# Opening steps of both mixture-of-experts stages reordered in a Flamingo-style block kernel

## The chip, the cores and the metric

The kernel is written in Bass, with every engine's instruction list and every semaphore set by hand. It runs on one core of one Trainium2 chip. The metric is the device time of the whole program in microseconds (us); less is better. Five engines work side by side: PE (TensorE, with PEld for its weight loads), DVE (VectorE), ACT (ScalarE), POOL (GpSimd) and SP (SyncE, which here only issues DMAs; SPq is its queue).

## The reference

x is 128 sequences of 64 rows of 128 numbers, 8192 rows in all. Four layers follow each other, and each adds a gated attention and a gated feed-forward part to x. The two feed-forward parts that matter here are mixtures of eight experts with two chosen per row. The first (layer 0) normalises x, takes logits against `gate_w`, and gives the two largest a softmax weight; every expert is one 128x128 matrix. The second (layer 2) is this:

```python
logits = jnp.einsum('bne,ec->bnc', x, Wr) + br
probs = jax.nn.softmax(logits, axis=-1)
topk_probs, topk_idx = jax.lax.top_k(probs, TOP_K)
...
combine = jnp.einsum('tk,tke->te', flat_w, onehot)
out = jnp.zeros_like(flat_x)
for ei in range(NUM_EXPERTS):
    h = jax.nn.gelu(flat_x @ W1[ei] + b1[ei], approximate=False)
    y = h @ W2[ei] + b2[ei]
    out = out + combine[:, ei:ei + 1] * y
...
x = x + jnp.tanh(g_ffn[0]) * _L0_ffn_ref(_layernorm(x, axis=-1), L0_ffn_gate_w, L0_ffn_We)
x = x + jnp.tanh(g_ffn[2]) * _L2_ffn_ref(_layernorm(x, axis=-1), L2_ffn_Wr, ...)
```

Both kernels compute every expert for every row and multiply by the coefficient, which is zero where the expert was not chosen.

## The kernel before

x stays on the chip for the whole run, as 64 tiles of 128 rows. Eight stages come one after another: attention0, experts0, attention1, spiking1, attention2, experts2, attention3, quantised3. Each stage begins on every engine with a wait for the last row update of the stage before, so a stage that ends earlier lets all that follows start earlier.

A mixture stage goes over 16 groups of 4 tiles (512 rows) in a software pipeline. A loop written out by hand calls `body(at)` for each step s, and `at(k)` is group s+k, or nothing where that group does not exist. So `at(4)` is a group four steps ahead of the one whose outputs are made, and the first steps, in which `at(0)` is nothing, are the opening: only their front parts have work. Every engine works through its own `body` strictly in the order of the text, and waits where a semaphore says so. The order of the work is nothing but these lists.

**First mixture, experts0 (lines 830 to 1008), opening steps -4 to -1.** A group goes through these stations:
- DVE takes the statistics of its four tiles (L712, L718); POOL turns the variances into 1/sqrt (L738, L741); DVE makes the shift -mean/sigma (L972); ACT makes the normalised rows (L1000); PE transposes them (L917) and ACT copies the result to xT (L1005).
- One step later PE makes the logits (L901). DVE copies them (L926) and runs `top_two` (L695 to L705, L932); ACT makes two sigmoids of the gap (L989); DVE makes the coefficients (L937, L942).
- One step later PE transposes the coefficients (L908) and ACT copies them (L994, the "ct copy"). SP stores them to DRAM (L864, 16 KB), waits until they are there, and issues the spread (L868), which brings them back to all 128 partitions (2048 KB in SBUF).
- One step later DVE weighs: xT times the spread coefficients, eight instructions of 128x512 (L952). Then PE sums over the experts (L888, `outputs`) and DVE updates x (L963).

Before the change DVE's `body` has the order statistics of the new group, update of the old one, `top_two`, shift of the new group, first three weighings, coefficients, other five. ACT has sigmoids, ct copy, normalised rows, xT copy. PE has outputs of the first tile, logits, transpose of the coefficients, outputs of the other three tiles, transposes of the new group.

**Second mixture, experts2 (lines 1579 to 1779), opening steps -3 to -1.** It is the same idea with three groups ahead. `t_front` and `a_front` (L749, L754) transpose a normalised group and copy it. `scores` (L1683 to L1688) follows the logits (L1655), ACT makes the exponential (L1768), and `routing` (L1694 to L1708) ends in the coefficients, which PE transposes (L1668). ACT's ct copy is L1774, the store L1609, the spread L1613. PE then multiplies the coefficients with the output bias (L1673) into the bank that the next group's logits use, and DVE adds it to x (L1749, semaphore `b2_added`). The inner layer has 12 chunks: PE `hidden` (L1633, three chunks per call, three banks in turn), ACT the Gelu out of the bank (`hidden_out`, L1758), DVE the product with the coefficients (`weigh`, L1720). PE's `outputs` is L1643. On PE `t_front` stands at the end of each step and `hidden` in quarters q = 0 to 3, with the transpose of the coefficients behind q = 1. On ACT the ct copy stands behind the third quarter's Gelus and `a_front` at the end of the step. On DVE the statistics, the first weighing and the normalised rows (L202) of the new group all stand ahead of `routing`.

Of the kernel before, what the change touches and what calls it, by code (L numbers as in the profile page):

```python
# [20 lines left out]
P = 128  # L21
# [808 lines left out]
def experts0(k, no):  # L830
# [50 lines left out]
    def tensor(pe):  # L881
# [11 lines left out]
        def body(at):  # L893
            if g := at(0):
                outputs(g, 0)
            if g := at(3):
# [7 lines left out]
            if g := at(2):  # L904
                pe.wait_ge(*s["coef"](g))
                if g.has(1):
                    pe.wait_ge(*s["ct_sb"](g.back(1)))
                pe.transpose(ps[0:COLS, COEFT, 0:P], coef[g.par], k.ident).then_inc(s["ct_psum"].sem, 1)  # L908
# [12 lines left out]
    def vector(dve):  # L921
# [22 lines left out]

        def weigh(g, first, last):
# [9 lines left out]
        def body(at):  # L955
# [5 lines left out]
            if old:  # L961
# [3 lines left out]
                    .then_inc(f["x_updated"].sem, GROUP)  # L965
            if far:
                top_two(far)
            if new:
                dve.wait_ge(*f["rstd_ready"](sub(new, GROUP - 1)))
                if new.has(1):  # L970
                    dve.wait_ge(*f["xhat_ready"](sub(new.back(1), GROUP - 1)))
                dve.scalar_tensor_tensor(out=shift, in0=k.mv[:, :, 0, 0], scalar=-1.0, in1=k.rstd[:, :, 0],  # L972
                                         op0=ALU.mult, op1=ALU.mult).then_inc(s["shift"].sem, 1)
# [8 lines left out]
    def scalar(act):  # L982
        def body(at):
            if g := at(3):
                act.wait_ge(*s["gap"](g))
                if g.has(1):
                    act.wait_ge(*s["part"](g.back(1)))
                for n in range(2):
                    act.activation(share[:, n], gap, ACT.Sigmoid, scale=2.0 * n - 1.0).then_inc(s["share"].sem, 1)  # L989
            if g := at(2):  # L990
# [3 lines left out]
                act.activation(coefT[g.par][0:COLS, :], ps[0:COLS, COEFT, 0:P], ACT.Copy).then_inc(s["ct_sb"].sem, 1)  # L994
            if g := at(4):
# [583 lines left out]
def experts2(k, no):  # L1579
# [44 lines left out]
    def tensor(pe):  # L1624
# [23 lines left out]
        def body(at):  # L1648
            g, nxt, far = at(0), at(1), at(2)
            if far:  # L1650
# [25 lines left out]
            if at(3):  # L1676
                t_front(pe, at(3))
        steps(pe, G, 3, 0, body)

    def vector(dve):  # L1680
# [41 lines left out]

        def body(at):
            old, nxt, far, new = at(-1), at(1), at(2), at(3)
            if far:
                scores(far)
# [453 lines left out]
```

## Time and profile before

| what | value |
|---|---|
| time, 3 runs | median 2242.03 us, 2236.01 to 2242.62 |
| the profiled execution | 2245.91 us, span 2244.1 us |
| mean granted clock of TensorE | 0.944 of full speed |
| PE busy | 1965.8 us, 88% of the span |
| DVE busy | 1700.4 us, 76% |
| ACT busy | 1192.8 us, 53% |
| POOL busy | 262.5 us, 12% |
| experts0 in the span | about 672 to 853 us |
| experts2 in the span | about 1378 to 1795 us |

"Busy" is the time in which an engine worked on an instruction, "idle" what lies between. In a timeline row stand the start in us, the duration, the engine, the line, the operation, output <- input with shapes, the count of merged instructions, and in brackets the idle time before it with what ended it. A windows row has the stretch, its length, then busy time and count of PE, PEld, DVE, ACT and POOL, the granted clock of PE (1.00 is 2.4 GHz, 0.50 is 1.2 GHz), the DMA share and GB/s. A wait marked "issue" has no releaser that the profile could name. Matmul times are modelled at their ends, and a matmul in float32 stands there as two instructions.

### The profile page before, as it was taken

Reading aid. Unit: us, or ns where it says so; the run is one execution under the profiler, and the core shown is the slowest. Engines: PE = TensorE matmul, PEld = TensorE weight load, DVE = VectorE, ACT = ScalarE, POOL = GpSimd, SP = SyncE. Lnnn points to the kernel's source line nnn. Section 1 sums busy time; section 2 is a strip of 40 time slices with the busy share of each in tenths; the row PEclk is TensorE's granted clock in tenths of the full one; section 3 lists DMA queues with packets and bytes.
Section 4 is the critical chain, followed back from the end, with each engine's and each line's share of the span. In section 5 each row is a group of like instructions: output and inputs, shape, how many; then the busy total and the mean of one; then the engine's idle time right before and its main releaser. Section 6 shows DMA issues by size and latency. Waiting matters only on the chain. (4 is left out here: it accounts for less than half of the span.)

```text
span 2244.1 us, 48290 instructions
## 1 busy us (share of the span) xinstructions
PE 1965.8 (88%) x18173; PEld 1522.7 (68%) x18173; DVE 1700.4 (76%) x4753; ACT 1192.8 (53%) x2324; POOL 262.5 (12%) x553
## 2 busy tenths in 40 slices
PE   3999999999986998999989886999999986499808
PEld 3788888888876897777757665577777765244307
DVE  2787887878866887999967786766666668787894
ACT  1555555555543215888866553544454445316844
POOL 0011111011101101111111142000000022200000
PEclk9999999999997998999989998999999998699958
DMA  6222221212213551111100011222221111001462
GB/s 184 50 49 49 51 50 47 51 49 50 51 32 152 227 228 26 32 33 30 33 8 1 10 48 55 78 77 103 87 76 76 76 43 34 0 1 72 172 205 76
DMA packets 123591, 155.71 MB, mean 69 GB/s; under 512 B 47561, under 2 KB 104290, under 8 KB 119266
## 3 DMA queue, kind: packets, MB, share of 16 engines
q1 hardware_dynamic: 117368, 149.92, 20.8%
q8 instruction: 147, 2.41, 0.5%
q10 hardware_dynamic: 5994, 2.70, 0.4%
q14 instruction: 82, 0.67, 0.1%
HBM read 110.11 MB, written 25.69 MB: 61 GB/s over the span
## 5 line engine op out<-in xcount | busy, mean ns | idle before, releaser
L1720 DVE TENSOR_TENSOR arena<-arena 128x512 f32<-128x512 f32 (+1 forms) x256 | 170.7, 685 | 68.9 <-ACT arena L1758 64.8
L1758 ACT ACTIVATE arena<-banks,b1c 128x512 f32<-128x512 f32 x192 | 131.7, 687 | 170.4 <-PE banks L1633 170.2
L1643 PEld LDWEIGHTS banks<-w2a,arena 128*128 128x128 f32 x1024 | 124.1, 192 | 28.6 <-issue 28.6
L888 PE MATMUL banks<-we,arena 128*128 128x128 f32 x1024 | 132.9, 284 | 4.4 <-DVE arena L952 0.5
L491 PE MATMUL banks<-arena,wk 128*128 128x128 f32 x1024 | 134.5, 286 | 1.1 <-DVE arena L609 1.1
L888 PEld LDWEIGHTS banks<-we,arena 128*128 128x128 f32 x1024 | 122.5, 195 | 12.8 <-DVE arena L952 12.4
L491 PEld LDWEIGHTS banks<-arena,wk 128*128 128x128 f32 x1024 | 122.1, 196 | 12.4 <-issue 10.7
L1643 PE MATMUL banks<-w2a,arena 128*128 128x128 f32 x1024 | 124.7, 275 | 0.0
L595 DVE TENSOR_TENSOR arena<-arena,konst 128x512 f32<-128x512 f32 x64 | 44.3, 693 | 104.3 <-DMA arena<-arena 104.3
L1633 PE MATMUL banks<-arena,w1s 128*128 128x512 f32 x256 | 122.1, 611 | 0.0
L501 PE MATMUL banks<-wv,arena 128*128 128x512 f32 x256 | 120.9, 595 | 0.0
L638 ACT ACTIVATE arena<-banks 128x512 f32<-128x512 f32 x64 | 38.2, 597 | 142.0 <-PE banks L491 142.0
L202 DVE TENSOR_SCALAR xhat<-x_tiles,mean_var,rstd 128x128 f32<-128x128 f32 x256 | 79.2, 341 | 34.5 <-POOL rstd L741 26.4
L738 POOL TENSOR_SCALAR var_eps<-mean_var 128x4 f32<-128x4 f32 x96 | 22.0, 229 | 702.7 <-DVE mean_var L718 700.5
L741 POOL TENSOR_TENSOR rstd<-var_eps,konst 128x4 f32<-128x4 f32 x96 | 100.1, 1043 | 15.3 <-POOL var_eps L738 11.7
L1850 PE MATMUL banks<-konst,local_max 128*1 128x128 f32 (+1 forms) x4 | 1.4, 348 | 111.0 <-DVE local_max L1834 111.0
L632 ACT ACTIVATE arena<-arena 128x512 f32<-128x512 f32 x128 | 80.6, 630 | 25.7 <-DVE arena L579 24.9
L1893 PE MATMUL banks<-arena,wup 128*128 128x512 f32 x192 | 92.0, 617 | 0.8 <-ACT arena L2051 0.8
L579 DVE TENSOR_TENSOR arena<-banks,arena 128x512 f32<-128x512 f32 x128 | 88.5, 691 | 4.4
L1198 ACT ACTIVATE arena<-arena 128x512 f32<-128x512 f32 x128 | 80.7, 630 | 16.2 <-DVE arena L1152 11.4
L1147 DVE TENSOR_REDUCE arena<-banks 128x8 f32<-128x512 f32 x128 | 87.3, 682 | 2.4 <-PE banks L1084 2.3
L952 DVE TENSOR_TENSOR arena<-arena 128x512 f32<-128x512 f32 x128 | 79.6, 686 | 10.9 <-issue 9.4
(271 smaller groups left out, 5091.5 us busy)
## 6 DMA issues: line engine op xcount, KB each, us to landing
arena<-coef_scratch SPq DMA_DIRECT2D x32, 2048.0 KB, 7.2
arena<-arena SPq DMA_DIRECT2D x256, 64.0 KB, 2.0
gated_scratch<-arena SPq DMA_DIRECT2D x16, 768.0 KB, 3.2
arena<-gated_scratch SPq DMA_DIRECT2D x16, 768.0 KB, 4.4
arena<-z1T_scratch SPq DMA_DIRECT2D x128, 64.0 KB, 2.4
arena<-ctxT_scratch SPq DMA_DIRECT2D x32, 256.0 KB, 2.8
arena<-in_ctx SPq DMA_DIRECT2D x64, 64.0 KB, 1.9
z1T_scratch<-arena SPq DMA_DIRECT2D x64, 64.0 KB, 1.7
```

The source lines that it names most:

```text
L491: mm = pe.matmul(ps[:, n, c * P:(c + 1) * P], k.wk0[:, c * P:(c + 1) * P], Z[t.par][:, :, n], start=True, stop=True)
L501: mm = pe.matmul(ps[:, 4 + b, :], Z[t.par][:, b].rearrange("p s i -> p (s i)"), k.wv0[:, :], start=True, stop=True)
L579: dve.tensor_tensor(prob[:, o].rearrange("p (c n) -> p c n", c=HPAIRS), sc, m.unsqueeze(2).broadcast_to([P, HPAIRS, P]), ALU.subtract)\
L741: pool.tensor_tensor(k.rstd[:, :, 0], k.ve[:, :, 0], k.konst[:, C_MHALF:C_MHALF + GROUP], ALU.pow).then_inc(f["rstd_ready"].sem, GROUP)
L888: mm = pe.matmul(ps[:, OUT + g.par, j * D:(j + 1) * D], xs[g.par][:, n, j * P:(j + 1) * P], k.we0[:, n, :], start=n == 0, stop=n == EXPERT ...
L1147: dve.tensor_reduce(mx[:, n].rearrange("p (r h) -> p r h", r=2), scores(n), AX.X, ALU.max)\
L1198: act.activation(prob[t.par][:, n], prob[t.par][:, n], ACT.Exp, scale=HD1 ** -0.5)\
L1633: pe.matmul(ps[:, HID + c % NHID, :], w, xTg[g.par], start=True, stop=True).then_inc(s["h_psum"].sem, 1)
L1643: mm = pe.matmul(ps[:, OUT + g.par, j * D:(j + 1) * D], hT[g.par][:, c, j * P:(j + 1) * P], w, start=c == 0, stop=c == CHUNKS2 - 1)
L1720: dve.tensor_tensor(hT[g.par][rows, c, :], hT[g.par][rows, c, :], wide_coef[g.par][rows, e, :], ALU.mult).then_inc(s["scaled"].sem, 1)
L1758: act.activation(hT[g.par][:, c, :], ps[:, HID + c % NHID, :], ACT.Gelu, bias=k.b1c[:, c:c + 1])\
L1893: pe.matmul(ps[:, 1 + CHUNKS3 * n + c, :], w[:, c, :], xdT[:, g.idx, :], start=True, stop=True)\
```

## The change

In **experts0** PE transposes the coefficients of `at(2)` ahead of the logits of `at(3)`, in every step. ACT makes the ct copy ahead of the sigmoids, in every step. In the opening steps alone (no `at(0)`), DVE makes the new group's shift ahead of `top_two`, and ACT makes the new group's normalised rows ahead of the sigmoids.

In **experts2** only opening steps differ. DVE has an `opening` of its own: a group's statistics are taken one step sooner, its normalised rows come first, then `scores` and `routing`, then the next statistics or the weighings. In step -2 PE does `t_front` of group 1 and the first three hidden chunks of group 0 right behind the logits of group 0, and these are left out of step -1; ACT follows with `a_front` of group 1 and the three Gelus between the exponential and the ct copy. From step 0 on the order is that of before.

```diff
 experts0, tensor
+            if g := at(2):
+                pe.wait_ge(*s["coef"](g))
+                ...
+                pe.transpose(ps[0:COLS, COEFT, 0:P], coef[g.par], k.ident).then_inc(s["ct_psum"].sem, 1)
             if g := at(3):
                 pe.wait_ge(*f["xT_sb"](g))
 ...
-            if g := at(2):
-                pe.wait_ge(*s["coef"](g))
-                ...
 experts0, vector
+            if new and not at(0):
+                shifts(new)
             if far:
                 top_two(far)
-            if new:
-                dve.wait_ge(*f["rstd_ready"](sub(new, GROUP - 1)))
-                ...
+            if new and at(0):
+                shifts(new)
 experts0, scalar: ct copy of at(2), then
+            if at(3) and at(0):
+                shares(at(3))
             if g := at(4):
                 ... (wait for the shift, the four normalised tiles)
+            if at(3) and not at(0):
+                shares(at(3))
+            if g := at(4):
                 act.wait_ge(*f["xT_psum"](g))
 experts2, tensor
+            if at(3) and not nxt:
+                t_front(pe, at(3))
+            if far and far.idx == 0:
+                hidden(far, 0)
             for q in range(GROUP):
-                if nxt:
+                if nxt and (q or nxt.idx):
                     hidden(nxt, 3 * q)
 ...
-            if at(3):
+            if at(3) and nxt:
                 t_front(pe, at(3))
 experts2, vector
+        def opening(at):
+            nxt, far, new = at(1), at(2), at(3)
+            if new.idx == 0:
+                statistics(new)
+            normalised(new)
+            if far:
+                scores(far)
+                routing(far)
+            if not nxt:
+                statistics(at(4))
+            if nxt:
+                dve.wait_ge(*coef_spread(nxt))
+                for c in (0, 3, 6):
+                    weigh(nxt, c)
+            if far:
+                biased(far)
+            if nxt:
+                weigh(nxt, 9)
 ...
+            if not at(0) and not old:
+                opening(at)
+                return
 experts2, scalar
-                if nxt:
+                if nxt and (q or nxt.idx):
                     hidden_out(nxt, 3 * q)
                 if far and q == 0:
                     act.wait_ge(*s["shifted"](far))
                     act.activation(expd, shifted, ACT.Exp).then_inc(s["expd"].sem, 1)
+                    if not nxt:
+                        a_front(act, at(3))
+                        hidden_out(far, 0)
 ...
-            if at(3):
+            if at(3) and (nxt or not far):
                 a_front(act, at(3))
```

## Rows read from the trace of the kernel before

**Rows 1.** Windows: second mixture, 3.3 us of its opening, 25 us of its loop.

```profile
1418.00:1421.30 3.30, 3.30 (x5) 1.51 (x5) 1.12 (x2) 0.69 (x1) 0.00 (x0) 0.50 0.69 238
...
1450.00:1475.00 25.00, 24.31 (x145) 18.03 (x144) 16.98 (x54) 12.11 (x17) 1.69 (x2) 1.00 0.22 85
```

**Rows 2.** Timeline: first mixture, opening steps, all engines.

```profile
675.24 0.16 DVE L972 SCALAR_TENSOR_TENSOR arena<-mean_var,rstd 128x4 f32<-128x4 f32 x1 [1.70 <-POOL rstd L741]
...
681.00 0.19 DVE L926 COPY arena<-banks 128x32 f32<-128x32 f32 x1 [4.29 <-PE banks L901]
...
683.14 0.30 ACT L989 ACTIVATE arena<-arena 128x4 f32<-128x4 f32 x2 [2.81 <-DVE arena L932]
...
683.73 0.19 DVE L942 TENSOR_TENSOR arena<-arena 128x32 f32<-128x32 f32 x1
...
684.85 0.38 DVE L718 BATCH_NORM_AGGREGATE mean_var<-bn_parts 128x2 f32<-128x6 f32 x4
...
688.74 0.19 DVE L926 COPY arena<-banks 128x32 f32<-128x32 f32 x1 [3.52 <-PE banks L901]
...
692.84 0.35 SPq L868 DMA_DIRECT2D arena<-coef_scratch  x1
...
700.29 1.90 DVE L952 TENSOR_TENSOR arena<-arena 128x512 f32<-128x512 f32 x3 [1.47 <-DMA arena<-coef_scratch]
```

**Rows 3.** Timeline: first mixture, loop.

```profile
733.02 0.87 DVE L712 BATCH_NORM_STATS2 bn_parts<-x_tiles 128x6 f32<-128x128 f32 x4
...
733.48 0.96 PE L901 MATMUL banks<-wg,arena 128*128 128x8 f32 x8
...
734.29 0.27 PE L908 MATMUL banks<-konst,arena 128*32 128x128 f32 x1
...
734.96 0.18 DVE L926 COPY arena<-banks 128x32 f32<-128x32 f32 x1
...
742.23 0.86 DVE L712 BATCH_NORM_STATS2 bn_parts<-x_tiles 128x6 f32<-128x128 f32 x4
```

**Rows 4.** Waits, 706 to 830 us (waiter <- releaser: total us, times, longest).

```profile
DVE arena L952 <- issue: 4.6, 5, 2.4
```

**Rows 5.** The view of line L868, the spread of the first mixture.

```profile
DMA to landing us min/median/max: 6.9/7.3/8.9
```

**Rows 6.** Timeline: end of the first mixture, SP and PE.

```profile
831.45 0.32 SPq L864 DMA_DIRECT2D coef_scratch<-arena  x1
834.10 0.32 SPq L868 DMA_DIRECT2D arena<-coef_scratch  x1
...
830.95 19.26 PE L888 MATMUL banks<-we,arena 128*128 128x128 f32 x157
```

**Rows 7.** Timeline: second mixture, opening steps, all engines.

```profile
1386.20 0.23 ACT L1768 ACTIVATE arena<-arena 128x32 f32<-128x32 f32 x1 [2.64 <-DVE arena L1688]
...
1390.46 0.18 DVE L1694 TENSOR_REDUCE arena<-arena 128x4 f32<-128x32 f32 x1
...
1393.70 1.01 PE L1668 MATMUL banks<-konst,arena 128*8 128x128 f32 x4 [8.21 <-DVE arena L1708]
...
1395.41 0.29 SPq L1609 DMA_DIRECT2D coef_scratch<-arena  x1
...
1396.89 0.34 SPq L1613 DMA_DIRECT2D arena<-coef_scratch  x1
...
1399.19 1.87 PE L1655 MATMUL banks<-wr,arena 128*128 128x8 f32 x8 [0.69 <-ACT arena L754]
...
1400.92 7.04 PE L1633 MATMUL banks<-arena,w1s 128*128 128x512 f32 x12
```

**Rows 8.** Timeline: second mixture, step -1, PE behind the routing of group 1.

```profile
1410.79 0.80 PE L1668 MATMUL banks<-konst,arena 128*8 128x128 f32 x4 [2.84 <-DVE arena L1708]
1411.39 3.42 PE L1633 MATMUL banks<-arena,w1s 128*128 128x512 f32 x4
...
1416.91 1.21 PE L1673 MATMUL banks<-b2r,arena 8*128 8x128 f32 x8 [1.25 <-ACT arena L1774]
```

More of the change, by code:

```diff
@@ L895, in body @@
                 outputs(g, 0)
+            if g := at(2):
+                pe.wait_ge(*s["coef"](g))
+                if g.has(1):
+                    pe.wait_ge(*s["ct_sb"](g.back(1)))
+                pe.transpose(ps[0:COLS, COEFT, 0:P], coef[g.par], k.ident).then_inc(s["ct_psum"].sem, 1)
             if g := at(3):
@@ L943, in coefficients, with shifts @@
                 .then_inc(s["coef"].sem, 1)
+        def shifts(new):
+            dve.wait_ge(*f["rstd_ready"](sub(new, GROUP - 1)))
+            if new.has(1):
+                dve.wait_ge(*f["xhat_ready"](sub(new.back(1), GROUP - 1)))
+            dve.scalar_tensor_tensor(out=shift, in0=k.mv[:, :, 0, 0], scalar=-1.0, in1=k.rstd[:, :, 0],
+                                     op0=ALU.mult, op1=ALU.mult).then_inc(s["shift"].sem, 1)
         def weigh(g, first, last):
@@ L965, in body @@
                     .then_inc(f["x_updated"].sem, GROUP)
+            if new and not at(0):
+                shifts(new)
             if far:
                 top_two(far)
-            if new:
-                dve.wait_ge(*f["rstd_ready"](sub(new, GROUP - 1)))
[L970 to L973, printed above, removed]
+            if new and at(0):
+                shifts(new)
             if nxt:
@@ L982, in scalar, with shares @@
     def scalar(act):
-        def body(at):
[L984 to L989, printed above, removed]
+        def shares(g):
+            act.wait_ge(*s["gap"](g))
+            if g.has(1):
+                act.wait_ge(*s["part"](g.back(1)))
+            for n in range(2):
+                act.activation(share[:, n], gap, ACT.Sigmoid, scale=2.0 * n - 1.0).then_inc(s["share"].sem, 1)
+        def body(at):
             if g := at(2):
@@ L1721, in weigh, with statistics, normalised, biased @@
                                       ALU.mult).then_inc(s["scaled"].sem, 1)
+        def statistics(g):
+            for j in range(GROUP):
+                d_front.stats(dve, g, j)
+            d_front.aggr(dve, g)
+        def normalised(g):
+            for j in range(GROUP):
+                d_front.xhat(dve, g, j)
+        def biased(g):
+            dve.wait_ge(*s["b2_psum"](g))
+            dve.tensor_tensor(rows_of(g), ps[:, LOGITS, :], rows_of(g), ALU.add).then_inc(s["b2_added"].sem, 1)
+        def opening(at):
[16 more added lines that the diff above has]
+                weigh(nxt, 9)
         def body(at):
             old, nxt, far, new = at(-1), at(1), at(2), at(3)
+            if not at(0) and not old:
+                opening(at)
+                return
             if far:
@@ L1732, in body @@
             if new:
-                for j in range(GROUP):
-                    d_front.stats(dve, new, j)
-                d_front.aggr(dve, new)
+                statistics(new)
             if nxt:
@@ L1739, in body @@
             if new:
-                for j in range(GROUP):
-                    d_front.xhat(dve, new, j)
+                normalised(new)
             if far:
```

6 lines of the change are left out of this document (1 added, 5 removed).

## The prediction

> **What bounds the kernel now.** One engine list per stage decides, so I first looked, in the windows, for the engine that is full in the loop of each mixture stage, then in the timeline at the opening, where none is. In the loop of the second mixture PE works 24.31 of 25.00 us at the full clock [rows 1]. In the loop of the first DVE is the full one: a group takes 9.21 us from one start of statistics to the next, with no idle between [rows 3]. DVE is also the one that stalls: the waits show five stalls ahead of the weighing, 4.6 us in all, with no releaser named [rows 4]. The spread explains them: the store goes out, then the spread, which takes 6.9 to 8.9 us to land [rows 5]. With 1.5 us for the store [rows 7] and 7.3 for the spread that is 8.8 of the 9.21 us of a group, so any slow spread makes DVE wait. In the openings everything is a chain from engine to engine: the first weighing of the first mixture starts at 700.29 [rows 2], 25 us after its first shift; in the second mixture PE idles 2.84 us for the coefficients of group 1 and gets them at 1410.79 [rows 8]. Both loops are full behind their opening, and the stages are in series, so what an opening saves comes off the end.
>
> **First mixture, opening (steps -3 to -1).** Group 0 gains no start: its logits are what DVE waits for, and they are copied at 681.00 as today. Its coefficients are done at 683.92 (683.73 + 0.19) [rows 2]. Group 1's rows are normalised on ACT ahead of the sigmoids, from 679.1 on, so its logits are in by 686.4. DVE then has the statistics of group 2, done at 685.23 (684.85 + 0.38), and now waits 1.70 us for POOL and makes the shift, 0.16 (both from the first shift [rows 2]), before it may route group 1. This is the wait that the change adds; behind it stands all of `top_two`. So group 1 is copied at 687.0 and not at 688.74. One cycle on DVE is then 2.92 (copy to coefficients: 681.00 to 683.92) + 1.31 (statistics, 683.92 to 685.23) + 1.70 + 0.16 = about 6.0, where it was 7.74. Group 2 is copied at 693.0; routing takes 2.14 (681.00 to the sigmoids at 683.14), so weighing of group 0 may begin at 695.1. Its spread: coefficients 683.92, transpose 0.3 to 0.4, copy 0.3, store 1.5, issued at 686.3; it needs 7.45 (692.84 to 700.29 [rows 2]) and lands at 693.7, 1.4 us before it is wanted. POOL's list is unmoved, and SP's too but for its times. **Gain 5.2 us** (700.29 - 695.1). Were the spread late by those 1.4 us, nothing would be lost.
>
> **First mixture, loop.** The transpose (0.27) now stands ahead of the logits. Today the logits end at 734.44 (733.48 + 0.96) and DVE takes them at 734.96 [rows 3]: 0.5 us of cover in a group that has the row update ahead of it, so it is free there. Step 0 has no such update; I charge it 0.3. If all groups lost the 0.27 it would be 3.5. The ct copy no longer waits behind the sigmoids: today it runs some 3.5 us after its transpose. It comes so much sooner, yet the store gains less, because it stands behind the spread in flight: at the end a store sent at 831.45, with a spread under way, takes 2.65 us until the next spread is issued at 834.10 [rows 6], against 1.48 with an empty queue (1395.41 to 1396.89 [rows 7]). Even so the spread of a group goes out about 1.5 us behind the landing of the last, and every one lands some 3 us before it is wanted. That covers the longest of the five stalls, 2.4 us. Between 0 and 4.6 I take all, **4.6 us**, for 3 us is more than any of them. The stalls of the last two groups give nothing: PE is full there, 19.26 us in one piece [rows 6].
>
> Sum of the first mixture: 5.2 - 0.3 + 4.6 = **9.5 us**.
>
> **Second mixture, opening.** The statistics of group 1 are now taken in step -3, so its normalised rows are ready while PE does the logits of group 0. The exponential of group 0 still ends at 1386.43. Routing, held back until 1390.46 today, starts at once and takes 3.24 (1390.46 to 1393.70): coefficients at 1389.7 and not 1393.7 [rows 7]. On PE, though, something now stands ahead of their transpose: four transposes of group 1 (1.1) and three hidden chunks, from 1386.7. Six instructions take 3.5 (half of 7.04 [rows 7]) to 5.1 (1.5 times 3.42 [rows 8], all at 1.2 GHz); I take 4.6, since PE comes out of idling: ends 1391.3. So the transpose is 1.6 us late and the ct copy stands behind three Gelus on ACT: done at 1392.6. Then bias products 1.2 to 2.1, DVE's bias addition 0.8, and the logits of group 1 start at 1395.0 +- 0.5 and not at 1399.19. They end at 1396.6 (1.1 to 1.87), and from there to the coefficients it is 0.7 (scores) + 0.25 (exponential) + 3.24 with nothing of DVE's in between: **1400.7 and not 1410.7**. Meanwhile PE does chunks 3 to 5, 2.6 to 5.1 us, done by 1401.7 at the worst. From the transpose on, step -1 has its old order, so the 10 us last until step 0. The spread of group 0 goes out at 1394.1 and lands at 1401.2, 0.5 after the routing of group 1; DVE then has slack towards PE. ACT's table loads stay at the same count. **Gain 10.1 us**, from 9 (PE at 1.2 GHz and late) to 13 (at 2.4 GHz throughout). The loop of this stage is untouched.
>
> **The clock,** where I chose. PE idled only 1.25 us ahead of 1416.91, while the copy was made [rows 8], and yet ran at a granted 0.50 right behind, from 1418.00 to 1421.30 [rows 1]. The new order has two or three such short idles around the bias products, so I cost the chunks there near 1.2 GHz. The Trainium skill, in "TensorE: Matmul & The Clock Gate", section "Why this matters for your kernels", wants only long gaps between bursts avoided. By that rule short idles are harmless, the new opening would run at the full clock and the sum would be 3.5 us better; this trace speaks against it.
>
> **Sum.** 9.5 + 10.1 = 19.6 us. The profiled execution took 2245.9 and would take 2226.3; it lies 3.9 above the median of the three runs, 2242.0, from which I forecast 2242.0 - 19.6 = **2222.4 us**.
>
> **Rivals.**
> - *Loop stalls stay.* The five waits have another cause, or an earlier spread meets other traffic. For it: the profile names no releaser. Against: each lies where a spread is awaited. Gain 15.0: 2227.0. Chance 0.16.
> - *A poorer opening of the second mixture.* The hidden chunks hold up the transpose by their full 5.1 us, at each wait the clock falls again: 3 us less, 2225.4. Chance 0.10.
> - *Full clock,* by the skill's rule: 2218.9. Chance 0.10.
> - *No measurable gain.* One opening's chain is held by something I took for free (the spread, or POOL), and the loop loses the 3.5 us for the transposes: 19.6 - 10 - 3.5 = 6, 2236.0. Chance 0.05.
> - *Slower.* The clock falls inside the loop of the second mixture. PE idles 0.7 us per group there (24.31 of 25.00 [rows 1]) and keeps its full clock; were the new phase of the work to lose it once per group, a stretch of 3.3 us at half the clock [rows 1] costs 1.65 us, 16 times 26.4: 2242.0 - 19.6 + 26.4 = 2248.8. It decides from 12 such falls on. Against it: the loop's order is that of before. Chance 0.03.
>
> **How the numbers follow.** The forecast has 0.56 and is the likeliest. The first three rivals lie between 2218.9 and 2227.0; with 3 us for the scatter of the three runs and the bounds of the openings (4.2 below to 6 above) the range is 2214 to 2232, which leaves out the last two rivals and some tails. About 0.3%, 6.7 us, is what a measurement of this kernel can tell from no change, so faster means below 2235.3: 0.92. Within it 0.05, slower 0.03.
>
> **What would show it.** In the first mixture: shift before the copy of the logits on DVE in steps -3 to -1, the first weighing at 695 and not at 700.3, no stall ahead of L952's first weighing in the loop, DVE's copy of the logits without a wait. In the second: coefficients of group 0 at 1389.7, of group 1 ten us earlier counted from the first statistics, PE's loop still at 25.0 us a group. I would be wrong if a weighing still waits for its spread, if PE idles ahead of the logits in the loop, or if the second opening gets back its ten us in a wait for the coefficients of group 1 or for the bias addition.

## The result and the profile after

| | before | changed |
|---|---|---|
| median of the runs | 2242.32 us (4 runs, 2236.01 to 2243.92) | 2217.47 us (4 runs, 2215.18 to 2220.05) |
| ratio to before, 95% interval | | 0.9895 (0.9873 to 0.9917) |
| profiled execution | 2245.91 us, span 2244.1 | 2218.05 us, span 2216.3 |

The change saves 24.9 us of the medians; 19.6 were forecast (2222.4), with a range of 2214 to 2232. The same changed kernel, measured again later beside other runs of the kernel before, gave 2214.58 against 2236.25: 21.7 us, ratio 0.9917 (0.9893 to 0.9941).

The work is the same, as the first lines of the page of the changed kernel show (busy time, share of the span, instructions):

```profile
span 2216.3 us, 48290 instructions
...
PE 1958.5 (88%) x18173; PEld 1520.8 (69%) x18173; DVE 1700.1 (77%) x4753; ACT 1194.5 (54%) x2324; POOL 263.1 (12%) x553
```

PE is busy 7.3 us less (1965.8 before) with the same count of instructions. That is the clock, of which more below; the rest of the gain is waiting time.

To see where the time went I put marks into every trace: the first statistics (L712) of the first mixture, its first weighing, its last update of x; the first normalised rows (L202) of the second mixture, the last instruction that makes the coefficients of group 1, the first `outputs` matmul on PE that reads `w2b`, the last update; the end. `w2b` is read from the ninth chunk on, so the mark "outputs" lies 1.7 to 1.8 us behind the very first `outputs` matmul of the stage, in every kernel alike; differences between kernels are not touched by this. From the starts of these instructions come the stretches of this table. Some starts are known only to 0.1 us, so the second decimal of a stretch can be off by 5. "Opening" is first statistics to first weighing; "coef(1)" and "outputs" count from the first normalised rows of the second mixture.

| kernel | first mixture: opening | whole | between | second: coef(1) | outputs | whole | behind it |
|---|---|---|---|---|---|---|---|
| before | 28.15 | 180.25 | 528.1 | 29.96 | 48.58 | 424.18 | 439.4 |
| changed | 22.62 | 171.42 | 524.1 | 18.99 | 34.23 | 409.83 | 440.0 |

(us; a "whole" ends with the start of the last update.) The first mixture gives 8.8 us, its opening 5.5 of them; the second gives 14.35, all before the mark "outputs"; the remaining 4 to 5 us of this pair lie in stages that the change does not touch. In the timeline of the changed kernel the opening of the first mixture looks like this:

```profile
677.61 0.16 DVE L949 SCALAR_TENSOR_TENSOR arena<-mean_var,rstd 128x4 f32<-128x4 f32 x1 [2.06 <-POOL rstd L741]
...
679.83 0.19 DVE L926 COPY arena<-banks 128x32 f32<-128x32 f32 x1 [2.06 <-PE banks L906]
...
685.01 0.35 SPq L868 DMA_DIRECT2D arena<-coef_scratch  x1
685.64 0.16 DVE L949 SCALAR_TENSOR_TENSOR arena<-mean_var,rstd 128x4 f32<-128x4 f32 x1 [1.57 <-POOL rstd L741]
685.72 0.19 DVE L926 COPY arena<-banks 128x32 f32<-128x32 f32 x1
...
691.62 0.19 DVE L926 COPY arena<-banks 128x32 f32<-128x32 f32 x1
...
693.64 1.89 DVE L959 TENSOR_TENSOR arena<-arena 128x512 f32<-128x512 f32 x3
...
701.51 0.19 DVE L926 COPY arena<-banks 128x32 f32<-128x32 f32 x1 [1.30 <-PE banks L906]
```

The shift (L949 now) stands ahead of each copy of the logits, and DVE waits for POOL there: 2.06 us at the first, where before it stood 4.29 us for the logits anyway, and 1.57 us at the two others, as foretold. From copy to copy it is 5.9 us (679.83, 685.72, 691.62), where [rows 2] have 7.7. The first weighing has no idle ahead of it: its spread had landed. The last row is step 0: there DVE waits 1.30 us for the logits.

In the second mixture (the timeline again, all engines):

```profile
1372.54 0.23 ACT L1815 ACTIVATE arena<-arena 128x32 f32<-128x32 f32 x1 [3.03 <-DVE arena L1703]
...
1372.93 4.52 PE L1644 MATMUL banks<-arena,w1s 128*128 128x512 f32 x6
...
1375.74 0.25 DVE L1723 SCALAR_TENSOR_TENSOR arena<-arena,gates 128x32 f32<-128x32 f32 x1
...
1377.29 0.60 PE L1683 MATMUL banks<-konst,arena 128*8 128x128 f32 x4
...
1378.70 1.15 PE L1688 MATMUL banks<-b2r,arena 8*128 8x128 f32 x8 [0.81 <-ACT arena L1824]
...
1380.73 1.03 PE L1666 MATMUL banks<-wr,arena 128*128 128x8 f32 x8 [0.88 <-DVE x_tiles L1749]
...
1382.46 0.23 ACT L1815 ACTIVATE arena<-arena 128x32 f32<-128x32 f32 x1 [2.52 <-DVE arena L1703]
...
1385.77 0.60 PE L1683 MATMUL banks<-konst,arena 128*8 128x128 f32 x4 [1.33 <-DVE arena L1723]
1386.20 1.88 PE L1644 MATMUL banks<-arena,w1s 128*128 128x512 f32 x4
...
1390.19 1.15 PE L1688 MATMUL banks<-b2r,arena 8*128 8x128 f32 x8 [1.25 <-ACT arena L1824]
1391.27 2.84 PE L1644 MATMUL banks<-arena,w1tail 128*128 128x512 f32 x6
```

The coefficients of group 0 are there at 1375.99, but PE transposes them only at 1377.29, behind the hidden chunks: 1.3 us, forecast 1.6. From 1377 on everything on PE is short: the same four hidden instructions take 1.88 us and not 3.42, and bias products are again followed by a wait of 1.25 us, as in [rows 8], but not by a slow clock. Two windows of the changed kernel (length, then PE, PEld, DVE, ACT, POOL; the third number from the end is the granted clock), the first from step -1 of the second mixture, the other from step 0 of the first:

```profile
1390.20:1393.40 3.20, 3.20 (x13) 2.01 (x14) 3.17 (x6) 0.79 (x2) 0.00 (x0) 1.00 0.32 87
...
699.50:701.30 1.80, 1.80 (x11) 1.75 (x9) 0.56 (x5) 0.27 (x1) 0.76 (x2) 0.50 0.04 9
```

The first answers to the 0.50 of [rows 1]: here the clock helped. The second is the other side: the first mixture now reaches its logits of step 0 while PE still runs at 1.2 GHz. The first weighing moved from 700.3 to 693.6, but the clock came back at about the same time. Two windows of the kernel before, then two of the changed one:

```profile
700.80:704.40 3.60, 3.57 (x14) 3.10 (x14) 3.57 (x9) 0.60 (x1) 0.00 (x0) 0.50 0.80 294
704.60:707.00 2.40, 2.20 (x18) 1.82 (x18) 2.19 (x11) 0.00 (x0) 0.00 (x0) 1.00 0.89 375
...
701.50:704.00 2.50, 2.50 (x12) 2.50 (x13) 2.13 (x19) 0.35 (x3) 0.24 (x1) 0.50 0.59 210
704.20:707.00 2.80, 2.80 (x28) 2.80 (x27) 2.77 (x8) 1.29 (x4) 0.00 (x0) 1.00 0.99 415
```

In the kernel before, the first logits of the loop start at 705.94, at the full clock; in the changed kernel at 699.76.

### The profile page after: what moved, and what is told of

Same layout as the page of the kernel before. It is cut to its first block and busy times, and to the rows that moved or that the text cites. A ratio compares the mean times of both kernels' runs of the same rounds, so it can differ in the third digit from the quotient of the medians.

```text
span 2216.3 us, 48290 instructions
## 1 busy us (share of the span) xinstructions
PE 1958.5 (88%) x18173; PEld 1520.8 (69%) x18173; DVE 1700.1 (77%) x4753; ACT 1194.5 (54%) x2324; POOL 263.1 (12%) x553
## 5 line engine op out<-in xcount | busy, mean ns | idle before, releaser
L1735 DVE TENSOR_TENSOR arena<-arena 128x512 f32<-128x512 f32 (+1 forms) x256 | 170.3, 685 | 62.5 <-ACT arena L1805 57.7
L202 DVE TENSOR_SCALAR xhat<-x_tiles,mean_var,rstd 128x128 f32<-128x128 f32 x256 | 79.3, 342 | 35.4 <-POOL rstd L741 26.4
L738 POOL TENSOR_SCALAR var_eps<-mean_var 128x4 f32<-128x4 f32 x96 | 22.1, 230 | 680.1 <-DVE mean_var L718 677.9
L579 DVE TENSOR_TENSOR arena<-banks,arena 128x512 f32<-128x512 f32 x128 | 88.5, 692 | 4.4
L1163 DVE TENSOR_TENSOR arena<-banks,arena 128x512 f32<-128x512 f32 x128 | 87.5, 684 | 0.2
```

The costliest lines, as they stand in the source:

```text
L202: dve.tensor_scalar(k.xh[:, slot, :] if out is None else out, k.x[:, t.idx, :], k.mv[:, slot, 0, 0:1], k.rstd[:, slot, 0:1], ALU.subtract, ...
L579: dve.tensor_tensor(prob[:, o].rearrange("p (c n) -> p c n", c=HPAIRS), sc, m.unsqueeze(2).broadcast_to([P, HPAIRS, P]), ALU.subtract)\
L1735: dve.tensor_tensor(hT[g.par][rows, c, :], hT[g.par][rows, c, :], wide_coef[g.par][rows, e, :], ALU.mult).then_inc(s["scaled"].sem, 1)
```

## The experiments

Each kernel was timed beside the kernel before on the same chip. The table collects the stretches of all their profiled executions; the texts below quote what was written ahead of each.

| kernel | median, kernel before beside it | first: opening | whole | between | coef(1) | outputs | second: whole |
|---|---|---|---|---|---|---|---|
| first mixture alone | 2231.80, 2237.30 | 22.68 | 170.28 | 520.7 | 30.84 | 49.52 | 425.12 |
| second mixture alone | 2221.77, 2237.30 | 27.78 | 179.18 | 518.3 | 18.34 | 33.80 | 409.40 |
| openings alone | 2220.20, 2237.30 | 22.63 | 173.73 | 520.6 | 18.95 | 34.26 | 409.86 |
| logits first in the loop | 2217.11, 2237.30 | 22.65 | 170.65 | 523.7 | 18.96 | 34.28 | 409.78 |
| no early hidden chunks | 2226.74, 2239.36 | 22.68 | 172.88 | 523.2 | 25.18 | 43.74 | 419.34 |
| hidden chunks behind | 2224.27, 2239.36 | 22.71 | 172.61 | 522.6 | 21.16 | 38.11 | 413.71 |
| early hidden chunks alone | 2231.21, 2239.36 | 22.70 | 172.30 | 525.6 | 30.15 | 47.12 | 422.72 |
| before, idle filled | 2237.98, 2239.36 | 27.83 | 178.93 | 522.8 | 30.99 | 46.24 | 421.84 |
| changed, again | 2214.58, 2236.25 | 22.65 | 172.85 | 520.1 | 18.18 | 35.19 | 410.79 |
| statistics ahead too | 2216.03, 2236.25 | 22.02 | 169.42 | 520.2 | 18.95 | 34.25 | 409.85 |
| exponential ahead | 2219.44, 2236.25 | 22.69 | 170.59 | 521.1 | 19.77 | 39.28 | 414.88 |

**Each stage alone.** The kernel with the new order in the first mixture only:

```diff
 def experts2(k, no):    # the whole function as before the change
```

> Only the first mixture has the new order, the second that of before. Theory A (the trace read stage by stage: first mixture 8.9 us shorter from its first statistics to its last update, second 14.3, the other 4.5 us scatter between executions): first mixture 171.4 us between these points as in the changed kernel, second mixture as before, whole time 2242.3 - 9 = 2233 (2230 to 2237). Theory B (the 4.5 us elsewhere belong to the change): 2229 or less, with the stretch between the two mixtures some 4 us shorter than before.

Ratio 0.9966 (0.9946 to 0.9987), 5.5 us of the medians, with 2.9 to 12 us in the interval; the stage itself takes 170.28, some 9 us less than in two other kernels that have its old order (179.18 in this set and, one set later, 178.93). And the one with it in the second only:

```diff
 def experts0(k, no):    # the whole function as before the change
```

> Only the second mixture has the new order. Theory A: 10.9 us sooner coefficients of group 1 plus 3.4 us from a TensorE clock that stays at its full level, 14.3 in all: 2228 (2225 to 2231), first mixture 180 us from first statistics to last update. Rival C (the clock's 3.4 us are luck of one execution): coefficients of group 1 again 10.9 sooner, but PE at a granted 0.50 for a part of step -1, and only 11 to 12 us gained: 2231.

Ratio 0.9937 (0.9908 to 0.9967), 15.5 us of the medians. The second mixture takes 409.40 and 425.12 us with the new and the old order in this set. 5.5 and 15.5 are 21.0, against 21.7 and 24.9 for both changes together, so within the scatter the stages add up. Rival C does not hold for the gain: from the coefficients of group 1 to the outputs it is 15.5 us as in the changed kernel, although PE has a granted 0.50 from 1383.9 to 1387.1, around these coefficients. Theory A holds against B: the stretch between the two was 528.1 us in the profile of before and 518.3 to 525.6 in the others, with no relation to which order stood around it (the least, 518.3, is from a kernel with the old first mixture). The 4 us that this stretch gave in the first pair are scatter.

**The loop of the first mixture.** What PE and ACT do anew in every step was put back, the openings kept:

```diff
-            if g := at(2):                      # PE: transpose of the coefficients
+            if (g := at(2)) and not at(0):
 ...
+            if (g := at(2)) and at(0):          # behind the logits
 ...
-            if g := at(2):                      # ACT: ct copy
+            if (g := at(2)) and not at(0):
 ...
+            if (g := at(2)) and at(0):          # behind the sigmoids
```

> As the changed kernel, but in the loop of the first mixture PE has the logits ahead of the transpose again and ACT the sigmoids ahead of the coefficient copy, as before. Theory A (the early copy takes the waits for the spread away, 4.6 us, and the transpose costs some 1.5 us in steps 0 and 1): the first weighing again 22.7 us behind the first statistics, then DVE waits for the spread again, 2 to 5 us in the loop; first mixture 173 to 176 us, whole time 2219 to 2222. Rival D (the waits for the spread are gone because the opening gives the DMAs a lead, and the loop's order is worth nothing): no waits in the loop, first mixture 171 or less, whole time 2216 to 2218.

The second variant puts only PE's order back and keeps ACT's early copy:

```diff
-            if g := at(2):                      # PE: transpose of the coefficients
+            if (g := at(2)) and not at(0):
 ...
+            if (g := at(2)) and at(0):          # behind the logits
```

> As the changed kernel, but from step 0 on PE in the first mixture makes the logits ahead of the transpose of the coefficients; ACT's early copy stays. Theory A (the transpose and the slow clock hold up the logits in steps 0 and 1; DVE waits 1.3 and 0.6 us for them there): these waits fall to 0.9 and 0.2, the loop keeps its early spreads, first mixture 170.5 to 171.2, whole time 0.5 to 1 us below the changed kernel. Rival E (the logits are late only because PE runs at 1.2 GHz in step 0 whatever the order): no difference in the whole, waits for logits stay within 0.3 us.

Whole times: ratio 0.9925 (0.99 to 0.995) and 0.9907 (0.9874 to 0.9939). The waits view from 700 to 820 us, of the kernel with the openings alone (waiter <- releaser: us in total, times, longest),

```profile
DVE arena L931 <- PE banks L906: 3.5, 3, 1.7
DVE arena L964 <- issue: 1.5, 4, 0.7
```

of the one with the logits first,

```profile
DVE arena L931 <- PE banks L906: 3.5, 3, 1.6
```

and of the changed kernel

```profile
DVE arena L926 <- PE banks L906: 2.7, 3, 1.3
```

In the kernel before it is 4.6 us ahead of the weighing [rows 4] and, for the logits, from 706 to 830 us:

```profile
DVE arena L926 <- PE banks L901: 1.1, 2, 0.7
```

ACT's early copy is what takes the last stalls away: with it no weighing waits for its spread until the last two groups; without it four do, 1.5 us in all. That is less than before, so a part of theory D is true: the openings alone already leave fewer stalls. How many there were before varies, though: the 4.6 us of the profiled kernel before are the most of three executions with the old order of this stage; the other two have 3.7 (before, idle filled) and 2.6 (second mixture alone).

The logits are waited for in all three kernels, also where they come first: rival E. I had expected the opposite for the kernel with the logits first, that the waits fall to 0.9 and 0.2; they are 1.09 and 1.65 us. PE's order is worth little, but it shows: the wait in step 0 is 1.30 us in all seven executions with the transpose first and 1.09 in all three with the logits first, a later one 0.82 and 0.71, so 0.3 us in all. The rest comes from PE's clock, which is still at 1.2 GHz in step 0 (the eight logits instructions take 1.72 us, against 0.96 at the full clock [rows 3]). The wait in step 1 follows the moment at which the clock comes back. The changed kernel has it back at 704.1 and waits 0.59 us; the second execution of the same kernel, with its first weighing at 693.7 as well, has it back at 706.8 and waits 1.86:

```profile
699.50:706.70 7.20, 7.20 (x36) 7.14 (x36) 5.37 (x31) 2.11 (x7) 1.21 (x2) 0.50 0.60 253
...
712.75 0.19 DVE L926 COPY arena<-banks 128x32 f32<-128x32 f32 x1 [1.86 <-PE banks L906]
```

Over all seven executions with the changed order the waits for logits come to 2.7 to 4.0 us; the changed kernel's 2.7 are the least. First statistics to last update is 173.7 with the openings alone and 170.7 with the logits first; the seven lie from 170.3 to 172.9, with a mean of 171.8. So the early copy is worth 1.5 us by the stalls and 2 to 3 us by these totals; both rest on a single execution of the openings alone.

**The early hidden chunks.** They were put back into step -1, DVE's new order kept:

```diff
-            if far and far.idx == 0:            # PE, step -2
-                hidden(far, 0)
 ...
-                if nxt and (q or nxt.idx):      # PE and ACT
+                if nxt:
 ...
                         a_front(act, at(3))
-                        hidden_out(far, 0)
```

> As the changed kernel, but the first three hidden chunks of group 0 and their Gelus stay in step -1, so PE transposes the coefficients of group 0 as soon as they are there. Theory A (DVE's new order carries the opening of the second mixture, the chunks in step -2 mainly fill PE): coefficients of group 1 come 3 us sooner than in the changed kernel (16 us after the first normalised rows, not 19.0), but PE has six chunks in step -1 and the clock may be at 0.50 for them; first outputs 36 to 38 us behind the first normalised rows (changed kernel 34.3, before 48.6). Rival F (the early chunks are the gain): coefficients of group 1 not sooner, outputs at 40 or later. Whole time 2219 to 2222 by A, 2224 or more by F.

This was a miss. The coefficients of group 1 come at 25.2, later than in the changed kernel, not sooner, and outputs at 43.7 and 2226.7 us in all are the numbers of rival F. Whether its reason holds too is another question. The timeline of this kernel says what they wait for:

```profile
1383.71 0.19 DVE L1701 TENSOR_TENSOR arena<-arena 128x32 f32<-128x32 f32 x1
...
1388.05 1.28 ACT L1813 ACT_TABLE_LOAD   x1
1389.34 0.23 ACT L1813 ACTIVATE arena<-arena 128x32 f32<-128x32 f32 x1
...
1389.60 0.18 DVE L1707 TENSOR_REDUCE arena<-arena 128x4 f32<-128x32 f32 x1 [5.70 <-ACT arena L1813]
```

The scores of group 1 are ready at 1383.9, the exponential comes at 1389.34: ACT's list has three Gelus ahead of it, and they wait for PE's chunks, and a table load. DVE stands 5.7 us. To see whether it is this and not PE's six chunks, only ACT's list was changed on top:

```diff
             for q in range(GROUP):
-                if nxt:
+                if nxt and (q or nxt.idx):
                     hidden_out(nxt, 3 * q)
                 if far and q == 0:
 ...
                     act.activation(expd, shifted, ACT.Exp).then_inc(s["expd"].sem, 1)
+                    if nxt and nxt.idx == 0:
+                        hidden_out(nxt, 0)
```

> As the kernel without early hidden chunks (DVE's new order, three chunks of group 0 still in step -1), but in that step ACT makes the exponential of group 1 ahead of the three Gelus. Theory J (the exponential waits 5.4 us behind three Gelus and a table load, and this, not the work of PE, made the coefficients of group 1 late at 25.2 in place of 19.0): they come at 20 to 21 although PE has the same work as there. Since PE still has six chunks ahead of the transpose, the first outputs come only at 38 to 41 (43.7 there, 34.3 in the changed kernel). Rival K (PE's six chunks or the clock make them late): 23 or more.

Its timeline:

```profile
1380.49 0.23 ACT L1813 ACTIVATE arena<-arena 128x32 f32<-128x32 f32 x1 [5.55 <-DVE arena L1701]
...
1380.75 0.19 DVE L1707 TENSOR_REDUCE arena<-arena 128x4 f32<-128x32 f32 x1 [0.29 <-ACT arena L1813]
```

Coefficients at 19.8 (DVE starts on them at 1383.49), outputs at 39.3: theory J, in both numbers. One swap on ACT is worth 5.4 us at the coefficients and 4.5 at the outputs. The other 5 us between 39.3 and the changed kernel's 34.2 lie with PE:

```profile
1374.99 2.07 PE L1686 MATMUL banks<-b2r,arena 8*128 8x128 f32 x8 [0.68 <-ACT arena L1823]
1377.94 1.84 PE L1666 MATMUL banks<-wr,arena 128*128 128x8 f32 x8 [0.88 <-DVE x_tiles L1747]
1379.63 6.98 PE L1644 MATMUL banks<-arena,w1s 128*128 128x512 f32 x12
1386.45 0.60 PE L1681 MATMUL banks<-konst,arena 128*8 128x128 f32 x4
```

The three chunks of group 0 still stand ahead of the transpose, which starts 2.7 us after the coefficients are there. And the clock is at 0.50 until 1382.9, 19 us behind the first normalised rows; in the changed kernel it is back at 1376.5, 10 us behind them, while PE works on the early chunks. So the bias products take 2.07 us here and 1.15 there, the logits of group 1 take 1.84 and 1.03. The early chunks thus have two uses: they take the Gelus out of ACT's way, and the work behind them runs at the full clock. How the 5 us divide between the chunks and the clock was not measured apart.

**The other half alone.** DVE's order of before, PE's and ACT's new one:

```diff
-            if not at(0) and not old:
-                opening(at)
-                return
```

> As the changed kernel, but DVE in the second mixture keeps the order of before in the opening (no statistics a step ahead, routing behind the normalised rows and the first weighings). Theory A: coefficients of group 0 at 12.9 as before, of group 1 at 26 to 28, outputs at 41 to 45: most of the 14.3 us is lost, so DVE's order carries it. Rival F (the early chunks are the gain): outputs at 37 or sooner.

Coefficients of group 1 at 30.2, outputs at 47.1: later even than I expected of theory A. The coefficients are no sooner than before (29.96); the 1.5 us at the outputs lie behind them, where the clock is at 0.50 for 3.7 us and not for 6.8. DVE's rows of that step:

```profile
1393.57 1.90 DVE L1735 TENSOR_TENSOR arena<-arena 128x512 f32<-128x512 f32 x3 [3.39 <-DMA arena<-coef_scratch]
...
1396.40 0.19 DVE L1709 TENSOR_REDUCE arena<-arena 128x4 f32<-128x32 f32 x1
```

The exponential ends at 1389.14, but routing starts only at 1396.40, behind a wait of 3.39 us for the spread, three weighings and the normalised rows. Against the kernel before, DVE's order alone gives 4.8 us at the outputs (48.6 to 43.7), the early chunks alone 1.5; together 14.3. (The other execution with the wholly old order has its outputs at 49.5, so each of these can be a microsecond more.) Each half is held by what the other one takes away: with DVE's old order routing waits behind the weighings, and with ACT's old order behind the Gelus.

**The order of the two in step -2.** Chunks and Gelus behind the transpose and the copy:

```diff
-            if far and far.idx == 0:
-                hidden(far, 0)
 ...
                     mm.then_inc(s["ct_psum"].sem, 1)
+                    if far.idx == 0:
+                        hidden(far, 0)
 ...
                     act.activation(coefT[0:EXPERTS, :], ps[0:EXPERTS, COEFT, :], ACT.Copy).then_inc(s["ct_sb"].sem, 1)
+                    if far.idx == 0:
+                        hidden_out(far, 0)
```

> As the changed kernel, but the three early chunks and their Gelus stand behind the transpose and the copy of the coefficients of group 0, not ahead of them. Theory A (the chunks hold the transpose up by 1.3 us, and the Gelus ahead of the copy do no more): transpose 1.2 us sooner, but the bias products now stand behind the chunks, so the logits of group 1 gain nothing: coefficients of group 1 at 19 to 21, outputs 34 to 37. Rival G (the order of the two is worth the 1.3 us): coefficients of group 1 at 17.7, outputs at 33.

Theory A in kind, somewhat beyond its numbers: coefficients at 21.2, outputs at 38.1, 4 us worse. PE idles 2.9 us for the coefficients, and the bias products then wait for the chunks. Of the 4 us, 2.2 lie ahead of the coefficients of group 1 and 1.7 behind them, where this execution has a stretch at 0.50; as a repeat of the changed kernel below has one too, only the 2.2 are surely the order's. The 1.3 us by which the chunks hold up the transpose in the changed kernel are well spent.

**The clock.** The kernel before with matmuls that nobody needs in PE's idle time of step -1:

```diff
+        def filler(n):
+            for _ in range(n):
+                pe.matmul(ps[:, OUT + 1, :], k.w1s[:, 0, 0:P], xTg[0], start=True, stop=True)
 ...
                 if far and q == 1:
+                    if far.idx == 1:
+                        filler(3)
                     pe.wait_ge(*s["coef"](far))
 ...
                 if far and q == 2:
+                    if far.idx == 1:
+                        filler(1)
                     pe.wait_ge(*s["ct_sb"](far))
```

> The kernel before with four matmuls of 128x512 added on PE in step -1 of the second mixture, into a bank that nobody reads: three ahead of the wait for the coefficients of group 1, one ahead of the wait for their copy. They fill idle time of 2.84 and 1.25 us. Theory H (the last 3.3 us of the gain come from TensorE's clock, which falls behind idle time in the kernel before): granted clock 1.00 from the coefficients of group 1 on, and from these to the first outputs 15.3 us in place of 18.6, the stage 3 us shorter. Rival I (the 3.3 us are other work taken out of step -1, or the phase of the work): 18.6 or more, and the clock falls as before.

In its timeline L1627 is the filler and L1637 the hidden chunks:

```profile
1404.02 2.74 PE L1627 MATMUL banks<-arena,w1s 128*128 128x512 f32 x6
...
1407.09 1.88 PE L1637 MATMUL banks<-arena,w1s 128*128 128x512 f32 x4
...
1412.16 2.84 PE L1637 MATMUL banks<-arena,w1tail 128*128 128x512 f32 x6
```

Two of its windows, ahead of the bias products and behind them, with the clock third from the end:

```profile
1406.00:1409.30 3.30, 3.30 (x12) 1.39 (x11) 2.76 (x7) 1.62 (x4) 0.00 (x0) 1.00 0.00 0
...
1412.80:1416.10 3.30, 2.64 (x10) 1.16 (x8) 2.15 (x4) 2.43 (x4) 0.00 (x0) 1.00 0.83 318
```

From the coefficients of group 1 to the first outputs it is 46.24 - 30.99 = 15.25 us, where it was 48.58 - 29.96 = 18.62 in the kernel before and 18.68 in the one with the old second mixture. Theory H: more work on PE makes this stretch 3.4 us shorter, for the clock stays up; it is the length that the changed kernel has (34.23 - 18.99 = 15.24). The stage is 421.84, against 424.18 and 425.12 in the two kernels with the same order and no filler; their coefficients came at 29.96 and 30.84, here at 30.99. This rests on one execution with the filler against two without; that its phase was lucky is not excluded, as the next kernel shows. The whole time shows almost nothing of it: 0.9986 (0.9972 to 1.0).

**Once more, and further.** The changed kernel again:

> The changed kernel once more, for a second trace of it. If the clock at its full level in step -1 of the second mixture comes with the order: from the coefficients of group 1 to the first outputs 15.2 to 15.4 us again, stage 409 to 410. If it was the phase of one execution: up to 18.6 and 413. First mixture 170.3 to 172.9, opening 22.6 to 22.7.

PE in its timeline, steps -2 and -1 of the second mixture:

```profile
1378.34 4.52 PE L1644 MATMUL banks<-arena,w1s 128*128 128x512 f32 x6
...
1387.12 1.15 PE L1688 MATMUL banks<-b2r,arena 8*128 8x128 f32 x8 [1.25 <-ACT arena L1824]
1388.20 4.25 PE L1644 MATMUL banks<-arena,w1tail 128*128 128x512 f32 x6
```

A mixed answer. Here the chunks behind the same 1.25 us of idling take 4.25 and not 2.84, and the stretch from coefficients to outputs is 17.0; the stage is 1 us longer. In the other five executions with this very order of the stage it is 15.2 to 15.5. Four of these five keep 1.00 from step -2 on; the second mixture alone has its 0.50 from 1383.9 to 1387.1, and still needs only 15.5. So the full clock mostly comes with the order, but an execution may lose it.

Last, the one cost that the change had added, the wait for POOL ahead of each routing, was taken away, on the kernel with the logits first:

```diff
-            if new:                             # DVE
-                for j in range(GROUP):
-                    d_front.stats(dve, new, j)
-                d_front.aggr(dve, new)
+            if new and (at(0) or new.idx == 0):
+                statistics(new)
 ...
             if new and not at(0):
                 shifts(new)
+                if not nxt:
+                    statistics(at(5))
 ...
-            if at(3) and not at(0):             # ACT: the sigmoids
-                shares(at(3))
             if g := at(4):
                 act.wait_ge(*f["xT_psum"](g))
 ...
+            if at(3) and not at(0):
+                shares(at(3))
```

> Built on the kernel with the logits first in the loop. In the opening of the first mixture DVE also takes the statistics one step ahead, so that POOL works beside top_two and DVE no longer waits 1.57 us for it ahead of each routing, and ACT copies xT ahead of the sigmoids. If that wait is what sets the opening now: its cycle falls from 5.9 to about 5 us, the first weighing comes at 21.2 to 21.6 in place of 22.65, then held by the landing of its spread; first mixture 169.2 to 170. If the spread already sets it: 22.4 or more. Whole time 1 us below the kernel with the logits first, less than a measurement can tell.

DVE in its timeline, opening of the first mixture:

```profile
684.20 0.15 DVE L959 SCALAR_TENSOR_TENSOR arena<-mean_var,rstd 128x4 f32<-128x4 f32 x1
...
686.32 0.19 DVE L931 COPY arena<-banks 128x32 f32<-128x32 f32 x1 [0.66 <-PE banks L906]
...
693.85 1.90 DVE L969 TENSOR_TENSOR arena<-arena 128x512 f32<-128x512 f32 x3 [0.44 <-DMA arena<-coef_scratch]
```

The wait for POOL is gone (no idle ahead of the shift), the two cycles are 5.7 and 5.0 us, and the weighing now waits 0.44 us for the spread: its new bound. It comes at 22.0 to 22.1, later than the 21.2 to 21.6 expected, for the sigmoids of group 0 now stand behind the xT copy and a table load, which made its coefficients and thus its spread 0.7 us late (the spread is issued 14.8 us behind the first statistics, 14.0 in the changed kernel). The stage is the shortest of all, 169.42; the whole, 2216.03 with 0.9914 (0.9888 to 0.994), cannot be told from the changed kernel's 2214.58 beside it.

## Why the prediction was right, and where it was off

- **Opening of the first mixture: right.** Forecast 5.2 us; 28.15 to 22.62 in the first pair, 22.6 to 22.7 against 27.8 to 28.2 in all that kept or changed it. The new wait for POOL is there, at 1.57 us each of the two times that count (forecast 1.70), the cycle is 5.9 (forecast 6.0), and the spread is in before it is wanted.
- **Loop of the first mixture: the mechanism right, the sum too large.** The stalls for the spread are gone, as forecast; but the 4.6 us came from one execution, and two others of the old order have 3.7 and 2.6. The transpose's charge, "step 0 has no such update; I charge it 0.3", was about right: 0.2 us in step 0 and 0.1 in a later one. What the sum left out is PE's 1.2 GHz in steps 0 and 1, which I had costed only in the other stage: DVE waits 2.7 to 4.0 us for logits, 1.1 to 1.4 before. So one of my signs, "DVE's copy of the logits without a wait", did not come. The ct copy ran 2.5 to 3.4 us after its transpose in the loop before, not "some 3.5", and runs 0.3 after it now. From first weighing to last update it is 148.8 us against 152.1 in the first pair, and 149.2 against 151.5 in the means of seven and three executions: 2.4 to 3.3 us in place of 4.3.
- **Opening of the second mixture: the direction right, the clock wrong.** Forecast 10.1 us ("I cost the chunks there near 1.2 GHz"), measured 14.35. Coefficients of group 0 came 3.6 us sooner (forecast 4.0) and their transpose was held up 1.3 (forecast 1.6); coefficients of group 1 came 11.0 sooner (forecast 10.0). The other 3.4 us lie behind them, where I had written that "from the transpose on, step -1 has its old order, so the 10 us last". The order is the old one, but PE has more work ahead of it and less idle time (1.33 us for the coefficients, 2.84 before) and keeps 2.4 GHz; filling the idle time of the old kernel gave the same 3.4 us in its one execution. This was the rival "full clock" with its 3.5 us, to which I gave 0.10, and the first measurement of 2217.5 stands nearer to it (2218.9) than to the forecast. Its 3.5 us were nowhere worked out; from the forecast's own bound of 13 us at the full clock it would be 2.9. I had taken one row, idle 1.25 us and then 0.50, for a rule.
- **The reason for the 10 us was incomplete.** I put them down to the routing that starts at once and to nothing of DVE's in between. The runs show a second holder on ACT: the exponential of group 1 stood behind three Gelus, which is worth 5.4 us and goes only because the early chunks take the Gelus out of step -1. The sum held this without saying it. Where the text says that the early chunks make the transpose late, it saw their cost and not their uses, of which the second is the clock: back 10 us behind the first normalised rows, 19 us or more in the kernels without early chunks.
- **The rest.** No slower loop in the second mixture, no loss of the clock in it: from outputs to last update 375.6 us in both kernels (424.18 - 48.58, 409.83 - 34.23). The stretches in between are untouched.
- The terms as measured in the first pair, 8.8 + 14.35 = 23.2, stand between the two measured gains, 24.9 and 21.7; 5.2 - 0.3 + 4.6 + 10.1 was 19.6. The parts missed in both directions, the first mixture by -0.7 and the second by +4.25, so the mechanisms carried the forecast, but its nearness to the measurement is in part luck.

## What to carry to other kernels

When steps of an opening are reordered, follow each moved item through every engine's list: here the gain of DVE's new order appears only once ACT's exponential is out from behind the Gelus, and either half alone gives 1.5 or 4.8 of 14.3 us. A wait added on one engine (1.57 us for POOL, twice) can be cheap where it replaces a longer round through all engines. And price matmuls behind an opening at both clock levels, for the 3.4 us there are nearly all by which the traces missed the forecast (23.2 - 19.6 = 3.6).

## What the runs showed of the hardware beyond what was expected

- The same idle time of 1.25 us ahead of the bias products was followed by a granted 0.50 in the kernel before (1418.00 to 1421.30 [rows 1]) and in the second execution of the changed one (six instructions in 4.25 us), and by 1.00 in the first (2.84 us). Its length alone does not decide. With matmuls added in the idle time, the one execution traced kept the clock up, and the way from coefficients to outputs was 3.4 us shorter.
- The Trainium skill, "TensorE: Matmul & The Clock Gate", section "Why this matters for your kernels", asks, against drops in mid-kernel, that long idle gaps between matmul bursts be avoided. Four of the six executions with the new order of the second mixture agree, with short idles of 0.6 to 1.3 us and a granted 1.00 throughout step -1; the other two do not, and the kernel before lost the clock behind 2.84 and 1.25 us.
- In the loop of the first mixture, all three executions with the old order have one stretch of 3.4 us at a granted 0.50 (803.5 to 806.9 in the kernel before); none of the ten with the new opening has one. Why, no run shows.
- The stretch between the mixtures, the same instructions in every kernel, took 518.3 to 528.1 us. Differences of that size between single executions say nothing of a change; the marks inside the openings agree to 0.1 us where the clock is the same.
